# Down projection of a LoRA MLP: one accumulator of 512 columns and one of 64 in place of two of 288

## The chip, the cores and the metric

One core of one Trainium2 chip runs the whole program. The metric is the device time of one execution in microseconds; lower is better.

## The reference

The input x is (128 batches, 32 channels, 512 time steps), float32. Four residual steps follow one another:

- a state-space convolution along time: one kernel of 512 taps per channel, a skip term, and a mask by the length of the batch;
- two channel mixes, each with a 32x32 matrix picked per batch (the kernel folds them into one matrix per condition);
- a gated MLP with LoRA, which holds nearly all of the time:

```python
gate = lora_add(x @ W_gate.T, x, A_gate, B_gate)      # 512 -> 1376, per-batch A, B of rank 16
up   = lora_add(x @ W_up.T,   x, A_up,   B_up)
act  = silu(gate) * up
down = lora_add(act @ W_down.T, act, A_down, B_down)  # 1376 -> 512
# lora_add(base, inp, A, B) = base + 0.5 * (inp @ A.T) @ B.T
```

The down projection therefore makes two products of the same activations: act @ W_down.T, 512 columns wide, and act @ A_down.T. Four batches share a tile, each with its own A_down of rank 16, so the second product is computed for all four, 64 columns wide, and a mask keeps what belongs to each row's own batch.

## The kernel before

**Tiles.** A tile is four batches by 32 channels, 128 rows of 512; there are 32 tiles. The first two and the last two are written out, and the 28 between run in hardware loops of two tiles (parity p = 0 and 1). A front part of some 130 us computes the convolution kernel, folds the mixes, splits the weights and does the convolution.

**Precision.** A product of float32 values is computed as three matmuls of type fp32r ("passes"): high by high, high by low, low by high. ScalarE makes the high parts (a copy that rounds), VectorE or GpSimd the low ones (value minus high part). A matmul here names a stationary operand, 128 columns of activations loaded into the array, and a moving operand, the weights that stream past it; its cost grows with the columns of the latter.

**TensorE's work in a tile** (`tile_pe`, lines 1049 to 1079) is a hand-written order. The hidden dimension, 1376 wide, is cut into eleven blocks of 128 (the last has 96) in three groups q: q = 0 is three blocks (352 wide), q = 1 and q = 2 four blocks each (512 wide).

1. `chunk(p, 0, 0)`, line 984: 12 matmuls for the gate's q = 0, 480 columns wide, since the LoRA A of gate and up rides along; then four transposes of the previous tile's last activations (`a_turn`, line 1005); `chunk(p, 0, 1)`, 12 of 352 columns; then `down(t-1, 1-p, 2)`, line 1016: four blocks of the previous tile's down projection.
2. `lora_b` for q = 0 (line 994, 4 matmuls of 352), `chunk(p, 1, 0)` (12 of 512), three transposes, `chunk(p, 1, 1)`, `lora_b_down(t-1)` (lines 1038 and 1039), `lora_b` for q = 1.
3. `chunk(p, 2, 0)`, the channel mix of the next tile (`mix`, lines 972 to 975, 3 matmuls of 512), `down(t, p, 0)` (three blocks), four transposes, `chunk(p, 2, 1)`, `lora_b` for q = 2, `down(t, p, 1)` (four blocks).

**Down projection.** The buffers `wd_hi` and `wd_lo` hold, for each of the eleven blocks, 640 columns: 64 for LoRA A of the even tile, 512 of W_down, 64 for LoRA A of the odd tile. An even tile uses columns 0 to 575, an odd one 64 to 639. Either is 576 wide, more than the 512 of a PSUM bank, so it is cut into two halves of DH = 288, one in bank 6 and one in bank 7 (`acc[0]`, `acc[1]`). For each block and pass both halves are computed with the same stationary operand:

```python
for h in range(2):
    o = NAD * p + h * DH
    last = mm(acc[h], ats[a][0:m, ...], wds[b][0:m, j, o:o + DH], ...)
```

After `down(.., 2)` VectorE masks the 64 columns of the LoRA A product (`td_mask`, line 855) and turns them (`td_turn`, line 833), ScalarE and VectorE split them (`td_high`, line 596, `td_low`, line 860), and `lora_b_down` adds their product with LoRA B (`bdst`) to the 512 columns. These lie as 224 + 288 (p = 0) or 288 + 224 (p = 1) in the two banks, so it is four matmuls. `out_sum` (lines 869 and 870) adds the residual in two VectorE instructions, and SyncE stores the tile.

**Waits on the way.** `down(t, p, 1)` waits for `a_low(t, 1)` (VectorE, line 848), which stands in VectorE's order behind `x3_turn`, 16 small transposes of the next tile's input (line 815); these wait for the mix of the next tile through a ScalarE copy (line 545). TensorE waits for `out_sum` ahead of the mix.

**The end.** For the last tile the last group is computed by `down_half`, line 1027: first the half with the LoRA A columns (12 matmuls of 288), then the other (12 more), during which the other engines mask, turn and split the LoRA A product. `lora_b_down` and `out_sum` end the kernel.

Of the kernel before, what the change touches and what calls it, by code (L numbers as in the profile page):

```python
# [6 lines left out]
ALU = mybir.AluOpType  # L7
# [7 lines left out]
B, C, T = 128, 32, 512  # L15
# [4 lines left out]
P = 128  # L20
# [20 lines left out]
OFF_U = F + NAG  # L41
NAD = GB * RANK
DW = NAD + T + NAD
DH = (NAD + T) // 2
WA, WAD, WB, WBD = RANK * 2 * KT, RANK * FT, FT * 2 * P, T
WDJ = ((0, 4), (4, 8), (8, 11))
NW = 2 * KT + len(WDJ)
# [26 lines left out]
def cond_resid_kernel(nc, xT, x, lens, idx, ssm, dskip, cst, cstp, w1t, w2, wall, ta, tad, tb, tbd, out):  # L74
# [8 lines left out]
    with ctx:  # L83
        def sem(name):
            return ctx.enter_context(nc.semaphore(name))
# [4 lines left out]
        ps = ctx.enter_context(nc.psum_tensor("ps", [P, 8, 512], F32))  # L90
        gub = [ps[:, n, :] for n in range(4)]
        atp = ps[:, 4, :]
        misc = ps[:, 5, :]
        acc = [ps[:, 6 + n, 0:DH] for n in range(2)]
        yp = [ps[:, n, :] for n in range(4)]
        kp = [ps[0:UN, 6 + n, :] for n in range(2)]
        wmp = ps[0:C, 5, :]
# [69 lines left out]
        bdst = sb("bdst", [P, T], F32R)  # L167
        x3n = sb("x3n", [P, 2, T])
# [3 lines left out]
        ats = [sb("at_hi", [P, T], F32R), sb("at_lo", [P, T], F32R)]  # L172
# [3 lines left out]
        tdm = sb("tdm", [P, P])  # L176
        tdr = sb("tdr", [P, P])
        tds = [sb("td_hi", [P, P], F32R), sb("td_lo", [P, P], F32R)]
        outb = sb("outb", [P, T])
# [8 lines left out]
        s = {n: sem("s_" + n) for n in names}  # L188
# [8 lines left out]
        def u_pair(q):  # L197
            return (ub[:, q] if q < NUW else ua[:, q - NUW] if q < 2 * NUW else ux[:, q - 2 * NUW])
# [23 lines left out]
        def at_end(n):  # L222

            return x3s[n][:].rearrange("p k n -> p (k n)")
# [14 lines left out]
        def ad_slot(tile, p):  # L239
            o = (NAD + T) * p  # L240
            return tile[:, :, o:o + NAD]
# [404 lines left out]
        def _(dve):  # L646
# [52 lines left out]
            for lo, hi, turn, _, _ in parts:  # L699
                last = V.tensor_scalar(kk[:, lo:hi], xs[:, lo:hi], i2p, turn, ALU.mult, ALU.add)  # L700
# [5 lines left out]
            for lo, hi, _, top, bottom in parts:  # L706
                last = V.tensor_scalar(xs[:, lo:hi], xs[:, lo:hi], top, bottom, ALU.min, ALU.max)
# [68 lines left out]
            for n in range(2):  # L776
                dve.wait_ge(s["kps"], n + 1)
                last = V.tensor_scalar(kf[:].rearrange("i h j -> i (h j)")[:, n * 512:(n + 1) * 512], kp[n], 2.0,
                                       None, ALU.mult)
# [12 lines left out]
            for h in range(C):  # L792
                q = h // 2
# [7 lines left out]
            tt = V.tensor_tensor  # L801
# [48 lines left out]

            def td_mask(t, p):
                dve.wait_ge(s["td"], t + 1)
                cols = acc[0][:, 0:NAD] if p == 0 else acc[1][:, DH - NAD:DH]
                dup = [NAD, 2]
                tt(tdm[:].rearrange("p (n e) -> p n e", e=2), cols.unsqueeze(2).to_broadcast([P] + dup),
                   mask[:].unsqueeze(2).to_broadcast([P] + dup), ALU.mult).then_inc(s["tdm"], 1)

            def td_low(t):
# [3 lines left out]
            def out_sum(t, p, stored=None):  # L862
                dve.wait_ge(s["accd"], t + 1)
                if stored is not None:
                    dve.wait_ge(s["ost"], stored)
                cut = DH - NAD if p == 0 else DH
                left = acc[0][:, NAD:DH] if p == 0 else acc[0]
                right = acc[1] if p == 0 else acc[1][:, 0:DH - NAD]
                tt(outb[:, 0:cut], left, x3n[:, p, 0:cut], ALU.add)
                tt(outb[:, cut:T], right, x3n[:, p, cut:T], ALU.add).then_inc(s["evac"], 1)  # L870

            dve.wait_ge(s["x0"], 16 * (5 + GB))
            tt(xa[:], xa[:], xb[:], ALU.add).then_inc(s["xsum"], 1)
# [5 lines left out]
            def tile_dve(t, p, first=False, second=False, last=False):  # L879
                if not first:  # L880
                    act_mul(t - 1, 1 - p, 2)
                t_mask(t, p)
                t_turn(t)
                if not first:
                    a_low(t - 1, 2)
                t_low(t)
                if not first:
                    td_mask(t - 1, 1 - p)
                    td_turn(t - 1)
                act_mul(t, p, 0)  # L890
                if not first:
                    td_low(t - 1)
                a_low(t, 0)
                if not first:
                    out_sum(t - 1, 1 - p, None if second else (t - 1) * 16)
                act_mul(t, p, 1)
                if not last:
                    x3_turn(t + 1, 1 - p)
                a_low(t, 1)
                if not last:  # L900
                    x3_low(t + 1)
# [8 lines left out]
            act_mul(NT - 1, 1, 2)  # L910
            a_low(NT - 1, 2, (at_end(0), at_end(1)))
            td_mask(NT - 1, 1)
            td_turn(NT - 1)
            td_low(NT - 1)
            out_sum(NT - 1, 1, (NT - 1) * 16)


        @block.tensor
        def _(pe):
            mm = nc.tensor.matmul  # L920
# [4 lines left out]
            for c in range(NCOND):  # L925
                o = wmp[:, c * C:(c + 1) * C]
# [3 lines left out]
                last = mm(o, idc, idc, start=False, stop=True)  # L930
# [3 lines left out]
            for h in range(C):  # L934
                n, o = h // (C // 2), h % (C // 2) * UI
                last = mm(kp[n][:, o:o + UI], kk[:, h * UN:(h + 1) * UN],  # L936
                          xs[:, X_V + h * UI:X_V + (h + 1) * UI], start=True, stop=True)
# [16 lines left out]
            for h in range(C):  # L954
                q = h // 2
# [5 lines left out]
                for c in range(KT):  # L961
                    last = mm(yp[h % 4][:, c * P:T], u_pair(q)[:, h % 2, c * P:(c + 1) * P],  # L962
                              tr[:, q % NTP, h % 2, 0:T - c * P], start=(c == 0), stop=(c == KT - 1))
# [3 lines left out]
            wds = [wd_hi, wd_lo]  # L967
# [40 lines left out]
            def down(t, p, q, blocks=None):  # L1008
                pe.wait_ge(s["alo"], t * 3 + q + 1)
                j0, j1 = PAIRS[q]  # L1010
                for j in range(j0, j1) if blocks is None else blocks:
                    m = P if j < FT - 1 else FTAIL
                    for a, b in PASSES:
                        for h in range(2):
                            o = NAD * p + h * DH
                            last = mm(acc[h], ats[a][0:m, (j - j0) * P:(j - j0 + 1) * P], wds[b][0:m, j, o:o + DH],  # L1016
                                      start=(q == 0 and j == j0 and a + b == 0), stop=False, skip_group_check=True)
                if q == 2:
                    last.then_inc(s["td"], 1)

            def down_half(h, blocks):

                j0 = PAIRS[2][0]
                o = NAD + h * DH
                for j in blocks:
                    for a, b in PASSES:
                        last = mm(acc[h], at_end(a)[:, (j - j0) * P:(j - j0 + 1) * P], wds[b][:, j, o:o + DH],  # L1027
                                  start=False, stop=False, skip_group_check=True)
                return last

            def lora_b_down(t, p):
                pe.wait_ge(s["tdlo"], t + 1)
                pe.wait_ge(s["bdlo"], t + 1)
                cut = DH - NAD if p == 0 else DH
                left = acc[0][:, NAD:DH] if p == 0 else acc[0]
                right = acc[1] if p == 0 else acc[1][:, 0:DH - NAD]
                for a in range(2):
                    mm(left, tds[a][:], bdst[:, 0:cut], start=False, stop=(a == 1), skip_group_check=True)  # L1038
                    last = mm(right, tds[a][:], bdst[:, cut:T], start=False, stop=(a == 1), skip_group_check=True)  # L1039
                last.then_inc(s["accd"], 1)  # L1040

            keep_warm(atp, NW_MLP)
# [6 lines left out]
            def tile_pe(t, p, first=False, last=False):  # L1049
# [6 lines left out]
                if not first:  # L1056
                    down(t - 1, 1 - p, 2)
# [5 lines left out]
                if not first:  # L1063
                    lora_b_down(t - 1, 1 - p)
# [6 lines left out]
                if not last:  # L1071
                    mix(t + 1, 1 - p)
                pe.wait_ge(s["adlo"], t + 1)
                down(t, p, 0)
                a_turn(t, 1)
                chunk(p, 2, 1)
                lora_b(t, p, 2)
                if not last:
                    down(t, p, 1)
# [8 lines left out]
            j0, j1 = PAIRS[1]  # L1088
# [3 lines left out]
            pe.wait_ge(s["alo"], NT * 3)  # L1092
            j0, j1 = PAIRS[2]
            down_half(1, range(j0, j1)).then_inc(s["td"], 1)
            down_half(0, range(j0, j0 + 2))
            down_half(0, range(j0 + 2, j1))
            lora_b_down(NT - 1, 1)


# [77 lines left out]
```

## Time and profile before

| | |
|---|---|
| median of 3 runs | 1070.89 us (1070.21 to 1073.7) |
| the profiled execution's own time | 1069.72 us |
| its span in the profile | 1067.9 us |
| TensorE matmul busy | 1037.9 us (97%), 5922 instructions |
| TensorE weight load busy | 906.3 us (85%), 5922 instructions |
| VectorE, ScalarE, GpSimd busy | 46%, 38%, 45% |
| mean granted TensorE clock | 0.997 of full speed |

Matmuls overlap in the pipeline: a row's duration runs from its start to its modelled end, and the next one starts before that. What one costs the engine is the step from its start to the start of the next, which is read from the start times, or from the chain of waits, where the pieces do not overlap and their lengths add up.

### The profile page before, as it was taken

How to read it: one execution, taken by the hardware profiler on the slowest of the kernel's cores; microseconds unless marked ns; L12 is line 12 of the kernel's file. 1: busy time of each engine (PE TensorE's matmuls, PEld its weight loads, DVE VectorE, ACT ScalarE, POOL GpSimd, SP SyncE). 2: the span in 40 equal slices, each digit the busy share in tenths (PEclk: the TensorE clock that was granted, in tenths of full speed). 3: DMA queues.
4: the chain of work that ended last, by engine and by line, in shares of the span. 5: the costliest groups of instructions: out<-in, count | busy, mean ns of one | idle time of the engine just before them, and what ended most of it. 6: DMA issues, size and time to landing. Idle time of an engine off the chain costs nothing.

```text
span 1067.9 us, 19023 instructions
## 1 busy us (share of the span) xinstructions
PE 1037.9 (97%) x5922; PEld 906.3 (85%) x5922; DVE 490.4 (46%) x1095; ACT 402.1 (38%) x627; POOL 484.8 (45%) x301
## 2 busy tenths in 40 slices
PE   3999899999999999999999999999999999999998
PEld 3665688888898888888888988888888888888887
DVE  8333344545444445445454445454454444454442
ACT  7002234434433433344343334334443433443341
POOL 0605354545445444545454454445454544544441
PEclk9999899999999999999999999999999999999999
DMA  9799342424333343424243333434242433334320
GB/s 340 249 404 337 116 110 89 134 69 138 98 109 101 99 123 101 120 84 136 71 138 97 108 99 101 125 99 122 80 137 73 137 96 107 102 98 128 104 75 20
DMA packets 100980, 135.50 MB, mean 127 GB/s; under 512 B 26395, under 2 KB 59420, under 8 KB 100956
## 3 DMA queue, kind: packets, MB, share of 16 engines
q1 hardware_dynamic: 100380, 135.12, 41.3%
q8 instruction: 12, 0.20, 0.1%
q10 hardware_dynamic: 576, 0.08, 0.1%
q14 instruction: 12, 0.10, 0.0%
HBM read 118.11 MB, written 16.99 MB: 127 GB/s over the span
## 4 chain that ended last, share of the span: by engine, by line
PE 94%; DVE 3%; DMA 3%; issue 0%; ACT 0%; DVEq 0%; ACTq 0%
PE ps L984 47%; PE ps L1016 27%; PE ps L994 8%; PE ps L962 5%; PE ps L1005 4%; DMA x1p<-yo 2%; PE ps L1039 1%; PE ps L1038 1%; PE ps L975 1%; PE ps L972 1%; PE ps L973 1%; DVE x3r L815 0%; DMA tr<-kpad 0%; DVE xs L704 0%; PE ps L936 0%; PE ps L1027 0%
## 5 line engine op out<-in xcount | busy, mean ns | idle before, releaser
L984 PE MATMUL ps<-wg_hi,x_hi 128*128 128x512 f32 (+2 forms) x768 | 299.2, 390 | 4.6 <-DVE x_lo L805 4.6
L984 PE MATMUL ps<-wg_lo,x_hi 128*128 128x512 f32 (+2 forms) x768 | 291.7, 380 | 0.0
L984 PE MATMUL ps<-wg_hi,x_lo 128*128 128x512 f32 (+2 forms) x768 | 290.7, 379 | 0.0
L471 POOL TENSOR_TENSOR bst<-braw,bst 128x1024 fp32r<-128x1024 f32 (+1 forms) x96 | 212.7, 2215 | 90.7 <-ACT bst L572 90.7
L815 DVE STREAM_TRANSPOSE x3r<-x3n 32x128 f32<-32x128 f32 x512 | 155.0, 303 | 92.3 <-ACT x3n L545 85.8
L588 ACT ACTIVATE at_hi<-ps 128x512 fp32r<-128x512 f32 (+1 forms) x95 | 53.4, 562 | 315.1 <-PE ps L1005 315.1
L984 PEld LDWEIGHTS ps<-wg_hi,x_hi 128*128 128x128 f32 x768 | 145.1, 189 | 25.9 <-issue 4.7
L984 PEld LDWEIGHTS ps<-wg_hi,x_lo 128*128 128x128 f32 x768 | 145.1, 189 | 25.2
L984 PEld LDWEIGHTS ps<-wg_lo,x_hi 128*128 128x128 f32 x768 | 145.3, 189 | 20.4
L1016 PE MATMUL ps<-wd_hi,at_hi 128*128 128x288 f32 x696 | 151.9, 300 | 0.0
L1016 PE MATMUL ps<-wd_lo,at_hi 128*128 128x288 f32 x696 | 149.0, 296 | 0.0
L1016 PE MATMUL ps<-wd_hi,at_lo 128*128 128x288 f32 x696 | 148.5, 295 | 0.0
L1016 PEld LDWEIGHTS ps<-wd_hi,at_hi 128*128 128x128 f32 x696 | 113.4, 188 | 14.9 <-DVE at_lo L848 12.3
L461 POOL TENSOR_TENSOR wg_lo<-agraw,wg_hi 128x256 fp32r<-128x256 f32 x64 | 58.2, 930 | 147.5 <-ACT wg_hi L558 147.5
L466 POOL TENSOR_TENSOR wd_lo<-adraw,wd_hi 128x704 fp32r<-128x704 f32 x32 | 66.8, 2088 | 124.7 <-ACT wd_hi L565 124.7
L1016 PEld LDWEIGHTS ps<-wd_hi,at_lo 128*128 128x128 f32 x696 | 112.1, 189 | 0.0
L1016 PEld LDWEIGHTS ps<-wd_lo,at_hi 128*128 128x128 f32 x696 | 111.6, 188 | 0.0
L583 ACT ACTIVATE act_t<-ps 128x512 f32<-128x512 f32 (+1 forms) x96 | 52.6, 548 | 151.6 <-PE ps L994 151.6
L572 ACT ACTIVATE bst<-braw,odd 128x1024 fp32r<-128x1024 f32 (+1 forms) x96 | 103.1, 1073 | 0.0
L848 DVE TENSOR_TENSOR at_lo<-ps,at_hi 128x512 fp32r<-128x512 f32 (+1 forms) x95 | 61.5, 647 | 79.4 <-ACT at_hi L588 78.5
L452 POOL TENSOR_TENSOR x_raw<-x_raw,xb 128x512 f32<-128x512 f32 x31 | 40.0, 1292 | 127.5 <-DMA xb<-in_x 127.5
L842 DVE TENSOR_TENSOR act_t<-act_t,ps 128x512 f32<-128x512 f32 (+1 forms) x96 | 60.3, 628 | 46.4 <-ACT act_t L583 46.4
(147 smaller groups left out, 1184.6 us busy)
## 6 DMA issues: line engine op xcount, KB each, us to landing
braw<-in_tb SPq DMA_DIRECT2D x256, 128.0 KB, 2.7
braw<-in_tb SPq DMA_DIRECT2D x128, 96.0 KB, 2.4
adraw<-in_tad SPq DMA_DIRECT2D x128, 88.0 KB, 1.9
tr<-kpad SPq DMA_DIRECT2D x16, 512.0 KB, 6.9
x1p<-yo SPq DMA_DIRECT2D x16, 512.0 KB, 5.7
xb<-in_x SPq DMA_DIRECT2D x32, 256.0 KB, 2.8
agraw<-in_ta SPq DMA_DIRECT2D x128, 64.0 KB, 2.0
bdraw<-in_tbd SPq DMA_DIRECT2D x128, 64.0 KB, 2.2
```

Of the source, the lines that this page charges most:

```text
L461: last = sub(ag_view(wg_lo, u), ag_from(u), ag_view(wg_hi, u).bitcast(F32), ALU.subtract)
L466: sub(ad_view(wd_lo, p), ad_from(), ad_view(wd_hi, p).bitcast(F32), ALU.subtract).then_inc(s["adlo"], 1)
L471: sub(v, b_from(p, q), v.bitcast(F32), ALU.subtract).then_inc(s["blo"], 1)
L572: copy(b_view(p, q), b_from(p, q), ACT.Copy, scale=odd[:, 0:1]).then_inc(s["bhi"], 1)
L588: copy((ats[0] if to is None else to)[:, 0:n * P], atp[:, 0:n * P], ACT.Copy).then_inc(s["ahi"], 1)
L815: last = V.transpose(turned, part)
L842: tt(act_t[:, 0:w], act_t[:, 0:w], gub[2 * ((p + q) % 2) + 1][:, 0:w], ALU.mult).then_inc(s["mul"], 1)
L848: tt(lo[:, 0:n * P], atp[:, 0:n * P], hi[:, 0:n * P].bitcast(F32), ALU.subtract).then_inc(s["alo"], 1)
L962: last = mm(yp[h % 4][:, c * P:T], u_pair(q)[:, h % 2, c * P:(c + 1) * P], tr[:, q % NTP, h % 2, 0:T - c * P], start=(c == 0), stop=(c == ...
L984: last = mm(bank[:, 0:n], x3s[a][:, k, :], wgs[b][:, k, o:o + n], start=(k == 0 and a + b == 0), stop=False, skip_group_check=True)
L994: last = mm(gub[2 * ((p + q) % 2) + u][:, 0:w], ts2[a][:, u, :], bst[:, (p + q) % 2, u * n:u * n + w], start=False, stop=(a == 1), skip_gr ...
L1016: last = mm(acc[h], ats[a][0:m, (j - j0) * P:(j - j0 + 1) * P], wds[b][0:m, j, o:o + DH], start=(q == 0 and j == j0 and a + b == 0), stop= ...
```

## The change

The 576 columns of a block are no longer cut in the middle. The 512 columns of W_down go to bank 6 in one matmul, and the 64 of LoRA A to bank 7 in another. The LoRA B product for down becomes one matmul of 512 per part in place of two, `out_sum` one VectorE instruction in place of two, and `td_mask` reads bank 7. In `down_half` the first half is now 256 columns of W_down and, for each, the 64 of LoRA A; the second half is 256 columns. Loads, layouts, semaphores and the order of the stages are as before.

```diff
-DH = (NAD + T) // 2
...
-        acc = [ps[:, 6 + n, 0:DH] for n in range(2)]
+        acc = ps[:, 6, :]
+        ta_d = ps[:, 7, 0:NAD]
...
-                cols = acc[0][:, 0:NAD] if p == 0 else acc[1][:, DH - NAD:DH]
...
-                tt(outb[:, 0:cut], left, x3n[:, p, 0:cut], ALU.add)
-                tt(outb[:, cut:T], right, x3n[:, p, cut:T], ALU.add).then_inc(s["evac"], 1)
+                tt(outb[:], acc, x3n[:, p, :], ALU.add).then_inc(s["evac"], 1)
...
-                        for h in range(2):
-                            o = NAD * p + h * DH
-                            last = mm(acc[h], ats[a][0:m, (j - j0) * P:(j - j0 + 1) * P], wds[b][0:m, j, o:o + DH],
-                                      start=(q == 0 and j == j0 and a + b == 0), stop=False, skip_group_check=True)
+                        w = ats[a][0:m, (j - j0) * P:(j - j0 + 1) * P]
+                        first = q == 0 and j == j0 and a + b == 0
+                        mm(acc, w, wds[b][0:m, j, NAD:NAD + T], start=first, stop=False, skip_group_check=True)
+                        last = mm(ta_d, w, ad_slot(wds[b], p)[0:m, j], start=first, stop=False, skip_group_check=True)
...
-                o = NAD + h * DH
+                cols = slice(h * (T // 2), (h + 1) * (T // 2))
...
-                        last = mm(acc[h], at_end(a)[:, (j - j0) * P:(j - j0 + 1) * P], wds[b][:, j, o:o + DH],
-                                  start=False, stop=False, skip_group_check=True)
+                        w = at_end(a)[:, (j - j0) * P:(j - j0 + 1) * P]
+                        last = mm(acc[:, cols], w, wds[b][:, j, NAD:NAD + T][:, cols], start=False, stop=False,
+                                  skip_group_check=True)
+                        if h == 1:
+                            last = mm(ta_d, w, ad_slot(wds[b], 1)[:, j], start=False, stop=False, skip_group_check=True)
...
                 for a in range(2):
-                    mm(left, tds[a][:], bdst[:, 0:cut], start=False, stop=(a == 1), skip_group_check=True)
-                    last = mm(right, tds[a][:], bdst[:, cut:T], start=False, stop=(a == 1), skip_group_check=True)
+                    last = mm(acc, tds[a][:], bdst[:], start=False, stop=(a == 1), skip_group_check=True)
```

## Rows read from the trace of the kernel before

**Rows 1.** The page: instructions and busy time, granted clock, shares of the chain.
```profile
PE 1037.9 (97%) x5922; PEld 906.3 (85%) x5922; DVE 490.4 (46%) x1095; ACT 402.1 (38%) x627; POOL 484.8 (45%) x301
...
PEclk9999899999999999999999999999999999999999
...
PE ps L984 47%; PE ps L1016 27%; PE ps L994 8%; PE ps L962 5%; PE ps L1005 4%; DMA x1p<-yo 2%; PE ps L1039 1%; PE ps L1038 1%; PE ps L975 1%; PE ps L972 1%; PE ps L973 1%; DVE x3r L815 0%; DMA tr<-kpad 0%; DVE xs L704 0%; PE ps L936 0%; PE ps L1027 0%
```

**Rows 2.** Chain of waits inside one tile: start us, us, what.
```profile
507.31 3.20 PE ps L1016 x24
...
518.42 2.72 PE ps L984 x12
...
521.82 2.38 PE ps L1016 x18
524.20 0.44 PE ps L1005 x4
524.64 2.78 PE ps L984 x12
527.42 0.93 PE ps L994 x4
528.35 3.42 PE ps L1016 x24
```

**Rows 3.** Who waited for whom: us in total, times, longest us.
```profile
PEld ps L1016 <- DVE at_lo L848: 12.3, 31, 0.4
```

**Rows 4.** Timeline, last transposes of a tile and the matmuls of 512 behind them.
```profile
524.37 0.19 PEld L984 LDWEIGHTS ps<-wg_hi,x_hi 128*128 128x128 f32 x1
524.40 0.47 PE L984 MATMUL ps<-wg_hi,x_hi 128*128 128x512 f32 x1
524.48 0.19 PEld L984 LDWEIGHTS ps<-wg_lo,x_hi 128*128 128x128 f32 x1
...
524.71 0.39 PE L984 MATMUL ps<-wg_lo,x_hi 128*128 128x512 f32 x1
524.71 0.19 PEld L984 LDWEIGHTS ps<-wg_hi,x_lo 128*128 128x128 f32 x1
```

**Rows 5.** Timeline, `lora_b_down`: start us, us, engine, line, operation.
```profile
516.85 0.27 PE L1038 MATMUL ps<-bdst,td_hi 128*128 128x224 f32 x1
516.85 0.19 PEld L1039 LDWEIGHTS ps<-bdst,td_hi 128*128 128x128 f32 x1
516.95 0.30 PE L1039 MATMUL ps<-bdst,td_hi 128*128 128x288 f32 x1
516.96 0.19 PEld L1038 LDWEIGHTS ps<-bdst,td_lo 128*128 128x128 f32 x1
517.09 0.26 PE L1038 MATMUL ps<-bdst,td_lo 128*128 128x224 f32 x1
```

**Rows 6.** Chain of waits in the front part, matmuls of 32 columns.
```profile
25.98 3.05 PE ps L936 x57
```

**Rows 7.** Line 936, its instructions: duration ns min/median/max, first and last start, forms.
```profile
L936 PEld LDWEIGHTS ps<-xs,kk x64: 100/131/131, 25.4 to 28.7; 128*16 128x16 f32 x64
```

**Rows 8.** Timeline, VectorE's transposes of the next input and ScalarE's copy of the activations.
```profile
522.49 5.05 DVE L815 STREAM_TRANSPOSE x3r<-x3n 32x128 f32<-32x128 f32 x16 [2.71 <-ACT x3n L545]
...
524.68 0.60 ACT L588 ACTIVATE at_hi<-ps 128x512 fp32r<-128x512 f32 x1 [2.22 <-PE ps L1005]
```

**Rows 9.** Timeline, from the last tile's last group to the end.
```profile
1060.66 0.39 PE L1027 MATMUL ps<-wd_hi,x_hi 128*128 128x288 f32 x1
...
1063.81 0.29 PE L1027 MATMUL ps<-wd_hi,x_lo 128*128 128x288 f32 x1
1063.91 0.19 PEld L1038 LDWEIGHTS ps<-bdst,td_hi 128*128 128x128 f32 x1
...
1064.72 0.46 DVE L869 TENSOR_TENSOR outb<-ps,x3n 128x288 f32<-128x288 f32 x1 [0.85 <-PE ps L1039]
1065.09 0.38 DVE L870 TENSOR_TENSOR outb<-ps,x3n 128x224 f32<-128x224 f32 x1
```

More of the change, by code:

```diff
@@ L852, in td_mask @@
                 dve.wait_ge(s["td"], t + 1)
-                cols = acc[0][:, 0:NAD] if p == 0 else acc[1][:, DH - NAD:DH]
                 dup = [NAD, 2]
-                tt(tdm[:].rearrange("p (n e) -> p n e", e=2), cols.unsqueeze(2).to_broadcast([P] + dup),
+                tt(tdm[:].rearrange("p (n e) -> p n e", e=2), ta_d.unsqueeze(2).to_broadcast([P] + dup),
                    mask[:].unsqueeze(2).to_broadcast([P] + dup), ALU.mult).then_inc(s["tdm"], 1)
@@ L865, in out_sum @@
                     dve.wait_ge(s["ost"], stored)
-                cut = DH - NAD if p == 0 else DH
-                left = acc[0][:, NAD:DH] if p == 0 else acc[0]
-                right = acc[1] if p == 0 else acc[1][:, 0:DH - NAD]
-                tt(outb[:, 0:cut], left, x3n[:, p, 0:cut], ALU.add)
-                tt(outb[:, cut:T], right, x3n[:, p, cut:T], ALU.add).then_inc(s["evac"], 1)
+                tt(outb[:], acc, x3n[:, p, :], ALU.add).then_inc(s["evac"], 1)
             dve.wait_ge(s["x0"], 16 * (5 + GB))
@@ L1033, in lora_b_down @@
                 pe.wait_ge(s["bdlo"], t + 1)
-                cut = DH - NAD if p == 0 else DH
-                left = acc[0][:, NAD:DH] if p == 0 else acc[0]
-                right = acc[1] if p == 0 else acc[1][:, 0:DH - NAD]
                 for a in range(2):
-                    mm(left, tds[a][:], bdst[:, 0:cut], start=False, stop=(a == 1), skip_group_check=True)
-                    last = mm(right, tds[a][:], bdst[:, cut:T], start=False, stop=(a == 1), skip_group_check=True)
+                    last = mm(acc, tds[a][:], bdst[:], start=False, stop=(a == 1), skip_group_check=True)
                 last.then_inc(s["accd"], 1)
```

## The prediction

> **What bounds the kernel now.** I read the page first. TensorE's matmuls are busy for 97% of the span and its lines fill almost all of the chain, line 984 with 47% and line 1016, the down projection, with 27% [rows 1]. VectorE, ScalarE and GpSimd are each under half busy. So a tile lasts as long as TensorE's own instructions. There are as many weight loads as matmuls, 5922 each [rows 1]: the second matmul of a pair loads its stationary operand again although it is the one already in the array.
>
> The chain of waits comes next, since its pieces add up. Twelve matmuls of 512 columns take 2.72 or 2.78 us, 0.227 or 0.232 each; 18 of 288 take 2.38 and 24 take 3.20, or 0.132 and 0.133 each [rows 2]. A pair of 288 therefore costs 0.265 us, twice the mean of these two. The other group of 24 takes 3.42 [rows 2]: here TensorE waits for the low part of the activations, once per tile for 31 tiles [rows 3]. The 0.22 more is what this wait costs.
>
> Last comes the timeline with loads and matmuls side by side, for how short a matmul can be. Two things are to be seen. First, the load for the next matmul starts with the current matmul and never ahead of it: in the stream of 512 columns a load and a matmul share the start 524.71, with the step of 0.23 between matmuls, though the load could have begun sooner [rows 4]. So one load is in flight ahead, not two. Second, loads of 128 columns in fp32r never follow each other by less than 0.11 us, wherever something makes them come close. From 516.85 to 516.96 it is a matmul of 224 columns that is short: the matmuls step by 0.10, the loads by 0.11, and the following matmul of 288 then takes 0.14 in place of 0.13 [rows 5]. From 524.37 to 524.48 the loads again step by 0.11 [rows 4]. The 0.19 us printed beside a load is its latency, not its pace.
>
> **The change, part by part.**
>
> *The pair in `down`.* There are 33 pairs in a tile (eleven blocks, three passes), 1056 in all, of which 12 are in `down_half`; that leaves 1044. Columns and loads stay at 576 and two for each pair. What moves is which matmul each load hides behind. Now each load, 0.11, has a matmul of 0.132 above it and is free. After the change the 64-column matmul's load hides behind the 512, but the next pair's load can only start with the 64-column matmul and takes 0.11.
>
> No row has a 64-column matmul, so I bound it from both sides. By columns alone: 224 columns more cost 0.227 - 0.132 = 0.095, so 64 columns would cost 0.132 - 0.095 = 0.037. That is the floor if the load binds nothing, and it would leave the pair at 0.264. Matmuls of 32 columns do run at 0.054 each, 57 in 3.05 [rows 6], but their loads are 16 columns wide [rows 7], not 128. With a load of 128 columns the nearest rows are the 224-column matmul at 0.10 and the transposes of 128 columns at 0.11 (four in 0.44) [rows 2]. I take the step of the loads, 0.11. The place closest in form is the last transpose of four with the matmul of 512 behind it. That matmul is recorded at 524.40, only 0.03 behind the start of its own load, but lasts 0.47 in place of 0.39; from its load, which starts with the last transpose, at 524.37, to the second matmul of 512 at 524.71 it is 0.34 for a narrow slot and a wide one [rows 4]. With 512 columns at 0.227, the pace of the chunk just ahead of the mix, the pair is 0.337, which is 0.072 more than 0.265. Times 1044 this is +75.2 us.
>
> For the range: at least 0.227 + 0.095 = 0.322 (slightly under the 224-column matmul), at most 0.2325 (four in 0.93 [rows 2]) + 0.11 + the 0.01 by which a matmul behind a load-bound one was longer [rows 5], 0.3525. That is +59.5 to +91.4 us.
>
> The page "TensorE: Matmul & The Clock Gate" of the Trainium skill (section LDWEIGHTS) puts a load at its columns over 1.2 GHz, 107 ns for 128; the rows agree with 0.11. The same page's section Back-to-back issue gap gives an isolated matmul N/2.4 + 2.5 ns and 60 cycles up to 64 columns; by that the pair would go from 245 to 241 ns, about 4 us less in all, which would be rival 1 below. Its 122.5 ns for 288 columns is under the 0.132 of this trace.
>
> *The wait that goes.* `down(t, p, 0)` has nine pairs, which end 9 x 0.072 = 0.65 us later. They lie between the mix, which starts VectorE's 16 transposes and then the low part, and the matmul that waits for that low part. The wait costs 0.22, so it should go: -0.22 x 31 = -6.8 us. What is late next? The activations themselves come 0.65 later too (their transposes stand behind `down(t, p, 0)`), but ScalarE's copy of them ended at 525.28 and VectorE was at its transposes until 527.54 [rows 8]; that slack covers it. All other waits sit behind stretches of TensorE work that stay or grow. No DMA, queue or semaphore is moved.
>
> *LoRA B.* Four matmuls, 0.10 + 0.14 twice or 0.48 [rows 5], become two of 512, 0.454 to 0.465: about -0.02 us, 32 times, -0.7 us. VectorE's one sum in place of two, and the mask's other bank, lie beside TensorE's work except at the end: nothing.
>
> *The end.* The first 12 of `down_half` become 12 of 256 (0.12, between 0.10 for 224 and 0.13 for 288) each followed by one of 64 at 0.11: 0.23 in place of 0.132, +1.2 us. The 12 others shrink to 1.44 in total. From the end of the first half, near 1062.25 (12 x 0.132 behind 1060.66), the LoRA chain of VectorE and ScalarE lasts until the load at 1063.91, already 0.1 behind the last matmul, so at most 0.1 comes back; one VectorE sum for two saves 0.1 [rows 9]. Together +1.0.
>
> **Sum:** 75.2 - 6.8 - 0.7 + 1.0 = +68.7 us. The profiled execution took 1069.72, which gives 1138.4; it stands 1.2 under the median of 1070.89, so against the median it is 1139.6. I say 1139.
>
> **The rivals.**
>
> *1. The narrow matmul costs its columns alone* (not slower). The array would keep the equal stationary operand, or the queue would fetch two loads ahead, so that the next pair's load lay under the 512. Place: the step from the 64-column matmul to the next 512. Price: the pair at 0.264, the wait of 0.22 stays, LoRA B gives 0.7: about 1070, and with the step at 0.03 in place of 0.037 some 7 us less, 1062. It decides if that step is under about 0.038. For it: 32-column matmuls at 0.054, though with narrow loads. Against it: loads equal matmuls in number even now, when half are repeats, and no load in these streams starts before the matmul ahead of it. Chance 0.08: same 0.05, faster 0.03.
>
> *2. Partly hidden.* The narrow step falls between 0.054 and 0.095, say 0.075 (a matmul may start before its load is complete, as the one recorded at 524.40 [rows 4]). Pair 0.302, +38.6 - 6.8: about 1103. Against it: the time came back in that matmul's longer duration. Chance 0.05.
>
> *3. The whole latency of the load is exposed,* 0.19: pair 0.417, +159 - 6.8, about 1223. Against it: with loads of 0.19 the 224-column matmul had a step of 0.10. Chance 0.03.
>
> *4. The clock falls in the down stages,* since 576 columns then fill less of the pair's time. The granted clock shows full speed in all but one slice, before the tiles begin [rows 1]. At the level of 1.2 GHz the 512 would cost about 0.44 and the pair 0.55: +298, about 1360. In the transposes, also narrow, it has not fallen. Chance 0.02.
>
> **How the numbers follow.** The forecast has 0.82. Its own range comes from the bounds: 59.5 - 6.8 + 0.3 = +53, or 1124, to +91.4 with the wait of 0.22 kept and +0.3, 1163. These two ends hold nearly all of the forecast's chance; the four rivals together are under 0.2, so the range is 1122 to 1162 and takes in none of them. A measurement of this kernel tells about 0.3% from no change. Slower by more than that is the forecast and rivals 2 to 4, 0.92; within it 0.05; faster 0.03.
>
> **What would show it.** In the profile after: matmuls and weight loads equal in number, 52 fewer (two fewer per tile for LoRA B, 12 more at the end); loads behind a 64-column matmul 0.11 after the load before them, and steps of matmuls that alternate near 0.23 and 0.11 (some records may show the 512 as early and longer); the 24 matmuls of a group of four blocks in about 4.04 us in the chain, the 18 of three blocks in 3.03; a tile 2.1 us longer; and no wait for the low part on TensorE in the loop. The prediction is wrong if the pair stays under 0.30, if there are fewer loads than matmuls, or if the granted clock shows half speed in the loop.

## The result, and the profile after

| | before | after |
|---|---|---|
| median | 1070.55 us (4 runs, 1069.31 to 1073.7) | 1139.92 us (4 runs, 1139.62 to 1142.38) |
| span of the profiled execution | 1067.9 us | 1137.8 us |
| matmuls, weight loads | 5922, 5922 | 5870, 5870 |
| mean granted clock | 0.997 | 0.999 |

The ratio is 1.0648, with a 95% interval of 1.0621 to 1.0676: slower by 69 us. The prediction had 1139, in a range of 1122 to 1162.

The page of the kernel after, in the parts that answer to [rows 1]. Lines 979, 1011 and 1012, 989, 1000 and 1033 are the former 984, 1016, 994, 1005 and 1038 with 1039.

```profile
PE 1106.9 (97%) x5870; PEld 938.1 (82%) x5870; DVE 482.1 (42%) x1063; ACT 402.2 (35%) x627; POOL 489.6 (43%) x301
...
PEclk9999999999999999999999999999999999999999
...
PE ps L979 44%; PE ps L1011 28%; PE ps L989 7%; PE ps L957 5%; PE ps L1000 3%; PE ps L1012 3%; DMA x1p<-yo 1%; PE ps L1033 1%; PE ps L967 1%; PE ps L970 1%; PE ps L968 1%; DVE x3r L815 0%; DMA tr<-kpad 0%; PE ps L1023 0%; DVE xs L704 0%; PE ps L931 0%
```

TensorE is as busy as before by its matmul row, 97%, although it takes 6.5% longer for 52 fewer matmuls. Every matmul still has its load, and the clock is full (0.999 in the mean). The busy share says nothing of the loss; the shares of the chain say where it is, since the down product has grown from 27% to 31% of a longer span.

The timeline of the kernel after in the down product: start us, us, engine, line, operation. PE is a matmul, PEld a weight load.

```profile
550.26 0.19 PE L1012 MATMUL ps<-wd_lo,at_hi 128*128 128x64 f32 x1
550.27 0.19 PEld L1011 LDWEIGHTS ps<-wd_hi,at_lo 128*128 128x128 f32 x1
550.29 0.47 PE L1011 MATMUL ps<-wd_hi,at_lo 128*128 128x512 f32 x1
550.38 0.19 PEld L1012 LDWEIGHTS ps<-wd_hi,at_lo 128*128 128x128 f32 x1
...
550.61 0.19 PE L1012 MATMUL ps<-wd_hi,at_lo 128*128 128x64 f32 x1
550.61 0.19 PEld L1011 LDWEIGHTS ps<-wd_hi,at_hi 128*128 128x128 f32 x1
550.64 0.47 PE L1011 MATMUL ps<-wd_hi,at_hi 128*128 128x512 f32 x1
550.72 0.19 PEld L1012 LDWEIGHTS ps<-wd_hi,at_hi 128*128 128x128 f32 x1
```

Read the loads, not the matmuls. The load for the wide matmul starts with the narrow one, 550.27, and the next load starts 0.11 behind it, 550.38; from there it is 0.23 to the load at 550.61. The matmul rows say something else: the wide one is recorded 0.03 behind the narrow one, and lasts 0.47 in place of the 0.39 of [rows 4]. Its recorded start is early, and the time for which the load holds it is booked as its duration.

The chain of the kernel after in the last group of a tile, which answers to the 24 matmuls in 3.42 us of [rows 2]: start us, us, what.

```profile
588.63 0.23 PE ps L1011
588.86 0.03 PE ps L1012
588.89 0.31 PE ps L1011
...
592.32 0.31 PE ps L1011
592.62 0.03 PE ps L1012
592.65 0.51 PE ps L979 x2
```

Between 588.89 and 592.32 lie ten pairs: 0.343 us each. The group starts without a wait: there is no row any more in which a weight load of TensorE waits for the low part. The chain also puts 0.03 on the narrow matmul and 0.31 on the wide one, for the same reason as above.

One tile in each kernel, from chunk to chunk, by the busy time of each engine in a stretch (stretch, length, then PE, PEld, DVE, ACT, POOL, granted clock, DMA share, GB/s), first after:

```profile
561.04:592.65 31.61, 31.61 (x167) 27.20 (x167) 13.43 (x30) 11.63 (x18) 15.90 (x10) 1.00 0.40 117
```

and before:

```profile
502.37:531.77 29.40, 29.40 (x169) 26.17 (x169) 13.49 (x32) 11.63 (x18) 13.66 (x9) 1.00 0.32 89
```

A tile is 2.21 us longer; 2.1 was predicted. VectorE and ScalarE do nearly the same work in it (13.43 us against 13.49, and 11.63 in both), and TensorE is the bound in both.

### The profile page after: what moved, and what is told of

It reads as the page before. It is cut to its first block, busy times and chain, and to the rows that moved or that the text cites. A ratio compares the mean times of both kernels' runs of the same rounds, so it can differ in the third digit from the quotient of the medians.

```text
span 1137.8 us, 18887 instructions
## 1 busy us (share of the span) xinstructions
PE 1106.9 (97%) x5870; PEld 938.1 (82%) x5870; DVE 482.1 (42%) x1063; ACT 402.2 (35%) x627; POOL 489.6 (43%) x301
## 4 chain that ended last, share of the span: by engine, by line
PE 94%; DVE 3%; DMA 2%; issue 0%; ACT 0%; ACTq 0%; DVEq 0%
PE ps L979 44%; PE ps L1011 28%; PE ps L989 7%; PE ps L957 5%; PE ps L1000 3%; PE ps L1012 3%; DMA x1p<-yo 1%; PE ps L1033 1%; PE ps L967 1%; PE ps L970 1%; PE ps L968 1%; DVE x3r L815 0%; DMA tr<-kpad 0%; PE ps L1023 0%; DVE xs L704 0%; PE ps L931 0%
## 5 line engine op out<-in xcount | busy, mean ns | idle before, releaser
L1011 PE MATMUL ps<-wd_lo,at_hi 128*128 128x512 f32 (+1 forms) x348 | 166.0, 477 | 0.0
L1011 PE MATMUL ps<-wd_hi,at_lo 128*128 128x512 f32 (+1 forms) x348 | 164.1, 472 | 0.0
L1011 PE MATMUL ps<-wd_hi,at_hi 128*128 128x512 f32 (+1 forms) x348 | 157.4, 452 | 0.0
L452 POOL TENSOR_TENSOR x_raw<-x_raw,xb 128x512 f32<-128x512 f32 x31 | 45.8, 1478 | 109.2 <-DMA xb<-in_x 109.1
L805 DVE TENSOR_TENSOR x_lo<-x3r,x_hi 128x512 fp32r<-128x512 f32 x32 | 67.1, 2097 | 45.1 <-ACT x_hi L551 45.1
L1011 PEld LDWEIGHTS ps<-wd_hi,at_lo 128*128 128x128 f32 (+1 forms) x348 | 65.1, 187 | 15.9
L1011 PEld LDWEIGHTS ps<-wd_lo,at_hi 128*128 128x128 f32 (+1 forms) x348 | 65.4, 188 | 14.4
```

Source lines behind the costliest of these rows:

```text
L805: tt(x3s[1][:].rearrange("p k n -> p (k n)"), x3r[:], x3s[0][:].rearrange("p k n -> p (k n)").bitcast(F32), ALU.subtract).then_inc(s["x3lo ...
L1011: mm(acc, w, wds[b][0:m, j, NAD:NAD + T], start=first, stop=False, skip_group_check=True)
```

## The experiments

Eight kernels, in two groups of four, each group on one chip beside the kernel before, which took 1069.27 us in the first group (the widened matmul, half the load for the wide one, the cut at 416, the subtraction moved) and 1071.41 in the second (the other four). Ratios are to the kernel before in the same group. The edits are cut to their main lines (`...` inside a line stands for arguments left as they are) and shown against the kernel named. In the texts put down before the runs, "load theory" is the prediction's mechanism: a matmul takes the larger of its columns and the weight load of the next matmul. "Column theory" is the rival by which only its columns count.

**A wider narrow matmul** (against the kernel after): 128 columns in place of 64, the other 64 unread.

```diff
-        mm(ta_d, w, ad_slot(wds[b], p)[0:m, j], ...)
+        mm(ta_w, w, wds[b][0:m, j, T * p:T * p + 2 * NAD], ...)      # ta_w: 128 columns of bank 7
```

> The changed kernel with the narrow matmul 128 columns wide in place of 64 (it also computes 64 neighbouring columns that nobody reads), 1056 times. Load theory: the step of the narrow matmul is the 0.108 us of the next pair's weight load, and 128 columns still fit under it, so nothing changes: 1140 us, within 3. Column theory (the narrow matmul pays for its columns and a fixed part): 64 more columns at 0.095/224 us each are 0.027 us, 1056 times, 1168 us.

Measured: 1139.24 us, ratio 1.0646 (1.0625 to 1.0668) to the kernel before. The 64 columns more, 1056 times, cost nothing: 1168 was the column theory's time. The timeline of this kernel:

```profile
553.22 0.22 PE L1013 MATMUL ps<-wd_lo,at_hi 128*128 128x128 f32 x1
553.22 0.19 PEld L1012 LDWEIGHTS ps<-wd_hi,at_lo 128*128 128x128 f32 x1
553.28 0.44 PE L1012 MATMUL ps<-wd_hi,at_lo 128*128 128x512 f32 x1
553.33 0.19 PEld L1013 LDWEIGHTS ps<-wd_hi,at_lo 128*128 128x128 f32 x1
...
553.56 0.22 PE L1013 MATMUL ps<-wd_hi,at_lo 128*128 128x128 f32 x1
```

The loads step by 0.11 as before, and narrow to narrow is 0.34. Only the recorded start of the wide matmul has moved, from 0.03 to 0.06 behind the narrow one, and its duration shrank from 0.47 to 0.44. Rival 1, a narrow matmul that pays for its columns, is out. A fixed minimum for a narrow matmul, whatever its load, is still possible; the next run asks for that.

**Half the load for the wide matmul** (against the kernel after): this leaves out rows 64 to 127 of the down product, but for the first matmul of each tile.

```diff
-        mm(acc, w, wds[b][0:m, j, NAD:NAD + T], start=first, ...)
+        n = P if first else P // 2
+        mm(acc[0:n], w[:, 0:n], wds[b][0:m, j, NAD:NAD + T], start=first, ...)
```

> The changed kernel with a stationary operand of 64 columns in place of 128 for the 512-column matmuls of the down product, but for the first of each tile; rows 64 to 127 of the down product are left out. Matmuls and moving columns stay. Load theory: the load that starts with each narrow matmul is halved, 0.054 us less per pair in some 1012 pairs, -55 us, and the wait for the low part (0.2 us per tile) comes back: about 1091 us. Theory of a minimum for a narrow matmul of its own, or of a cost of changing banks: the step stays at 0.11 and the time at 1140 us.

Measured: 1093.24 us, ratio 1.0212 (1.0189 to 1.0236), close to the 1091 of the load theory. The timeline of this kernel:

```profile
540.28 0.19 PE L1013 MATMUL ps<-wd_hi,at_hi 128*128 128x64 f32 x1
540.28 0.13 PEld L1012 LDWEIGHTS ps<-wd_lo,at_hi 128*64 128x64 f32 x1
540.31 0.42 PE L1012 MATMUL ps<-wd_lo,at_hi 128*64 128x512 f32 x1
540.34 0.19 PEld L1013 LDWEIGHTS ps<-wd_lo,at_hi 128*128 128x128 f32 x1
...
540.57 0.19 PE L1013 MATMUL ps<-wd_lo,at_hi 128*128 128x64 f32 x1
```

The same matmuls with the same moving columns are 46 us faster when the load under the narrow one has 64 columns: it steps by 0.06, and the pair by 0.29. A minimum of the narrow matmul's own, or a price for changing banks, would have left the time alone. The wide matmul now fills only half of the rows of its result, but that is not what saves: its slot, from the load at 540.34 to the narrow matmul at 540.57, is 0.23 as before, and all of the gain is in the narrow slot, 0.06 for 0.11. The wait for the low part is back as well, in part (who waited for whom in this kernel):

```profile
PEld ps L1012 <- DVE at_lo L848: 5.6, 31, 0.2
```

**Half the load for the narrow matmul** (against the kernel after): the mirror; this leaves out rows 64 to 127 of the LoRA A product.

```diff
-        last = mm(ta_d, w, ad_slot(wds[b], p)[0:m, j], start=first, ...)
+        n = P if first else P // 2
+        last = mm(ta_d[0:n], w[:, 0:n], ad_slot(wds[b], p)[0:m, j], start=first, ...)
```

> The changed kernel with a stationary operand of 64 columns in place of 128 for the 64-column matmuls of the down product, but for the first of each tile; rows 64 to 127 of the LoRA A product are left out. The mirror of the run with half the load for the wide matmul: here the shorter load is the one that lies under a matmul of 512 columns. Load theory: it was hidden already, so 1140 us, within 3. Theory that less loading or less work in a pair is what counts, wherever it stands: about 1093 us, as in that run.

Measured: 1144.22 us, ratio 1.0677 (1.064 to 1.0713), whose interval takes in the ratio of the kernel after. It is 4 us above the 1140 expected, so it misses the 3 us allowed, on the slow side. In the profiled execution (1147.66 us) most of the excess lies ahead of the tiles: the first load of the down product starts at 144.00 where it is 138.47 in the kernel after. The groups of nine and of twelve pairs are 0.01 and some 0.03 us longer by the starts of their loads, 2 us in all, and why is open. Halving a load that a matmul of 512 covers saves nothing, where halving the load under the narrow matmul gave 46 us. It matters where a load stands.

**Two narrow matmuls** (against the kernel after): twice 32 columns in place of 64.

```diff
-        last = mm(ta_d, w, ad_slot(wds[b], p)[0:m, j], start=first, ...)
+        for c in range(2):
+            last = mm(ta_d[:, c * 32:c * 32 + 32], w, ad_slot(wds[b], p)[0:m, j, c * 32:c * 32 + 32],
+                      start=first and c == 0, ...)
```

> The changed kernel with the 64 columns of LoRA A in two matmuls of 32, 1056 times; columns and results stay. Load theory: each narrow matmul costs a load, 0.108 us x 1056 = +114 us: 1254 us. Column theory with a fixed part of 0.013 us for a matmul: +14 us, 1154 us.

Measured: 1259.58 us, ratio 1.1761 (1.1722 to 1.1801). That is 120 us more than the kernel after, or 0.113 for each matmul added, with no column more. In its timeline the loads for the wide matmul start at 540.27 and 540.72, 0.45 for a wide and two narrow matmuls, where a pair took 0.34. The price of a narrow matmul here is about one load; the 120 us are 6 more than the 114 expected, and this rest is not explained.

**The cut at 416** (against the kernel before): 416 + 160.

```diff
-DH = (NAD + T) // 2
+DH = 416
+DR = NAD + T - DH      # the width of the second half, used where DH was
```

> The kernel before with its 576 columns cut at 416 in place of 288: 416 + 160. Load theory: 416 columns take about 0.187 us and the 160 are held at 0.108 by the load, a pair of 0.295 for 0.265: +31 us, the LoRA B product some 0.08 us more per tile (+3), the wait for the low part goes (-7): 1097 us. Column theory: the sum of columns is the same, 1071 us.

Measured: 1101.34 us, ratio 1.0295 (1.0269 to 1.0321), 32 us slower where 27 were expected (31 + 3 - 7). The 24 matmuls that took 3.20 take, in this kernel's chain:

```profile
520.10 3.59 PE ps L1017 x24
```

A pair is 0.299, and no load waits for the low part any more in this kernel either. The effect is not tied to a 64-column matmul, a whole bank or the layout of the change: a cut of the same 576 columns is enough, once one side is shorter than a load.

**The cut at 352** (against the kernel before): 352 + 224, the same edit.

> The kernel before with its 576 columns cut at 352 in place of 288: 352 + 224. Load theory: 352 columns take 0.158 us and 224 take 0.10 but are held at 0.108, a pair of 0.266 for 0.265, +1 us; the LoRA B product, in one parity 160 + 352, some 0.03 us more per tile, +1 us: 1072 us, within 2. A theory by which any uneven cut costs in proportion (31 us more at 416) would give about half of that, 1085 us.

Measured: 1075.43 us, ratio 1.0042 (1.0028 to 1.0056): 4 us slower, where the load theory had about 2 and the proportional one 14. The chain of this kernel has 3.25 for the 24 matmuls that took 3.20, and keeps the wait in the other group (3.47 for 3.42):

```profile
509.28 3.25 PE ps L1017 x24
...
530.46 3.47 PE ps L1017 x24
```

The pair costs 0.004 more in these groups, and 0.007 in the group of 18 (2.44 for 2.38), some 5 us in all, about the 4 measured. From 288 columns on the short side to 224 the time moves by 4 us, from there to 160 by 28 more: the edge lies near 224, where the theory puts it, though a cut near the edge already costs a little more than the larger of the two numbers.

**The subtraction moved** (against the kernel before): the low part between the 10th and 11th of VectorE's 16 transposes.

```diff
-                if not last:
-                    x3_turn(t + 1, 1 - p)
-                a_low(t, 1)
+                if last:
+                    a_low(t, 1)
+                else:
+                    x3_turn(t + 1, 1 - p, lambda: a_low(t, 1))     # called ahead of the 11th transpose
```

> The kernel before with VectorE's subtraction for the low part of the second group of activations moved between the 10th and the 11th of the 16 small transposes it stood behind. If the 0.22 us per tile in the chain are this wait, TensorE gains up to 0.22 x 31 = 6.8 us: 1064 us, if the six transposes behind it are not late for the next tile. If the wait only moves to the next tile's first chunk, or the 3.42 us are another effect, 1071 us.

Measured: 1063.51 us, ratio 0.9946 (0.9928 to 0.9964). It is 5.8 us faster than the kernel before, where up to 6.8 were expected, a gain of 0.5% that is small but clear of the noise, and it is the fastest of all kernels here. VectorE in its timeline:

```profile
520.13 3.14 DVE L817 STREAM_TRANSPOSE x3r<-x3n 32x128 f32<-32x128 f32 x10 [2.71 <-ACT x3n L545]
...
523.28 0.69 DVE L850 TENSOR_TENSOR at_lo<-ps,at_hi 128x512 fp32r<-128x512 f32 x1
...
524.00 1.90 DVE L817 STREAM_TRANSPOSE x3r<-x3n 32x128 f32<-32x128 f32 x6
```

and the group of 24 matmuls that took 3.42, in its chain:

```profile
525.99 3.20 PE ps L1019 x24
```

The wait is gone, and this kernel's profile has no row in which a load waits for the low part: the low part is ready at 523.97, two microseconds ahead of that group, and the last six transposes end in time for the next tile.

**The same move in the kernel after.**

> The changed kernel with VectorE's subtraction for the low part moved between the 10th and the 11th of the 16 small transposes, the edit that gave the kernel before 5.8 us. If the change had already taken that wait away, as the prediction's term of -6.8 us says, nothing is left to gain: 1140 us, within 3. If it had not, 1134 us.

Measured: 1140.42 us, ratio 1.0654 (1.0616 to 1.0692), no different from the kernel after. The edit that is worth 5.8 us in the kernel before is worth nothing here. The longer down product had taken the wait away.

## Why the prediction was right

**The pair.** This was the term that carried it, +75.2 us. A pair was put at 0.337: 0.227 for 512 columns and 0.11 for the load. The load's step is right to the last digit shown. What was short is the wide matmul: within a group a pair is 0.343 (ten in 3.43), which leaves 0.235 for it where I had taken the 0.227 of the chunk ahead of the mix. The first wide matmul of each group of 12 or 9 pairs follows a matmul of 352 or 512 columns and pays no load: the chain has 0.23 for it. In the tile shown above, the three groups take 4.03, 3.00 and 4.02 us in the chain, and what runs behind them 0.19 more than before, because the last narrow matmul's load is booked there (the chunk of 480 columns 2.68 for 2.60, the transposes 0.47 for 0.44, LoRA B of 352 0.72 for 0.64). That makes 11.24 for 33 pairs, 0.341 on average. The term comes out at 0.341 - 0.266 = 0.075 for each of 1044, +78 us.

**The wait that goes.** Predicted -6.8 us. It has no row in the profile after, the kernel before gains 5.8 us by losing it, and the kernel after gains nothing by the same edit. So the term stands, at about its size. Without it the forecast would have been 1146. The half-load run is a check of its other side: with nine pairs only 0.025 longer than before, a small wait was left, as this reasoning requires.

**LoRA B and the end.** Two matmuls of 512 take 0.47 in the chain where four took 0.49 in an even tile and 0.48 in an odd one: -0.5 us for -0.7. For the end I had +1.0. The first matmul of `down_half` starts at 1129.63 of a span of 1137.8, so 8.17 us remain; before it was 1060.66 of 1067.9, or 7.24 [rows 9]. That is +0.9.

**The sum.** 78 - 6.8 - 0.5 + 0.9 is +71.6, and the spans differ by 69.9. Of the rest, 0.6 lies ahead of the tiles: the mix of the second tile starts at 138.17 in the one profile and at 138.74 in the other, and nothing of the change stands before it. Some 1.1 us I can't place. The pair was 3 us too cheap in the sum, and these 1.7 us the other way came out against it, so the forecast was within 1 us of the median, closer than its parts: the mechanism was right, the last 2 us were luck.

**The rivals.** Rival 1 (columns alone) is refuted by the widened and by the doubled narrow matmul. The isolated formula in the section Back-to-back issue gap of the page "TensorE: Matmul & The Clock Gate" of the Trainium skill would have had the kernel some 4 us faster; that section itself says that the formula leaves the loads out and under-counts for few columns, and so it does here. The runs agree with the page's section LDWEIGHTS, whose 107 ns for a load of 128 columns is the 0.11 measured. Rival 2 (partly hidden) fails on its own observation: a matmul is indeed recorded as started before its load is through, but it gives the time back in its duration, and the pair is 0.34 whatever the recorded starts say. Rival 3 (the whole 0.19 of a load) would have been 1223, and a load added costs 0.113. Rival 4 fails on the granted clock, 0.999 in the mean and at 0.9 or more in every slice.

In none of the rows above does the next load start before the current matmul; where the current matmul stands behind a load-bound one and is recorded early, the load starts 0.09 behind it (550.29 and 550.38). Why it never comes sooner was not tried: an experiment that fetches two loads ahead, or keeps a stationary operand for two matmuls, was not made.

## What to carry to other kernels

Cost a matmul as the larger of two times: that of its moving columns, and that of the weight load that starts with it, which is the load of the next matmul. In fp32r with 128 weight columns that load steps by 0.11 us. So it matters little where columns are cut while each piece is about as long as that (288 + 288 and 352 + 224 differ by 4 us here), and a thin piece costs about a whole load however thin it is (64 or 128 columns the same, two of 32 cost two). A wait that an engine's order causes can be read off as the one group that is longer than its twins (3.42 against 3.20); look among the instructions ahead of its end for a place where the needed one could stand.

## What was not expected

The prediction allowed that some rows might show the matmul of 512 early and long. How regular this is was new: with a load-bound matmul ahead, the profile's recorded start of the following matmul is early by the part of the load that is not covered, 0.08 us here and 0.05 in the kernel with 128 narrow columns, and its duration is longer by as much. So the step from row to row and the chain put the loss on the wide matmul (0.31) and almost none on the narrow one (0.03) that causes it. Only the starts of the loads, or the step from narrow to narrow, show it right.

The cut at 352 costs some 0.005 us a pair more (0.271) than the sum of the two steps put down for it (0.266), although 224 columns are only 0.008 short of a load. Near the edge the larger of the two times is a little too low; why, no run here shows.

The only gain did not come from the change at all: moving one VectorE instruction took 5.8 us off the kernel before.
